# Cross-attention with masked image tokens: the setup of the first two query blocks in another order

## The reference

```python
text, ip_h = encoder_hidden_states[:, :end_pos], encoder_hidden_states[:, end_pos:]
q = _split_heads(hidden_states @ w_q, HEADS)
k, v = _split_heads(text @ w_k, HEADS), _split_heads(text @ w_v, HEADS)
out_text = _merge_heads(_sdpa(q, k, v))
mask_ip = _ip_mask(bbox, B, S, hidden_states.dtype)   # 0 or -10000 for each query and image token
k_ip, v_ip = _split_heads(ip_h @ w_k_ip, HEADS), _split_heads(ip_h @ w_v_ip, HEADS)
out_ip = _merge_heads(_sdpa(q, k_ip, v_ip, mask=mask_ip))
out = (out_text + out_ip) @ w_out + b_out + hidden_states
```

## Time and profile before

| | us |
|---|---|
| median of 3 runs (750.12 to 752.63) | 751.3 |
| the profiled execution | 747.52 |
| its span | 745.7 |
| PE busy | 690.5 (93%) |
| DVE busy | 537.3 (72%) |
| ACT busy | 288.2 (39%) |
| POOL busy | 213.6 (29%) |

### The profile page before, as it was taken

One profiled execution on the slowest core, in us unless ns is written; L12 is line 12 of the kernel. 1 busy time (PEld: TensorE's weight loads), 2 busy tenths in 40 slices (PEclk: granted clock), 3 DMA queues, 4 the chain that ended last, 5 costly groups with the idle time before them and its releaser, 6 DMA issues.

```text
span 745.7 us, 18922 instructions
## 1 busy us (share of the span) xinstructions
PE 690.5 (93%) x6410; PEld 630.2 (85%) x6410; DVE 537.3 (72%) x1686; ACT 288.2 (39%) x626; POOL 213.6 (29%) x359
## 2 busy tenths in 40 slices
PE   4977783899999999999999999999999999999987
PEld 3665363798999999999999999989898999999876
DVE  4342151978787888878787879797979787878764
ACT  1031112616262625353534444352626171616151
POOL 8100000523233231415050505051424242323323
PEclk9989796999999999999999999999999999999979
DMA  9946823335252625343434444444444343535220
GB/s 267 318 114 181 174 94 101 80 89 149 83 156 64 164 73 152 85 138 96 130 94 129 107 129 106 127 102 136 93 130 100 101 127 94 143 86 119 85 50 36
DMA packets 79543, 89.52 MB, mean 120 GB/s; under 512 B 10680, under 2 KB 63416, under 8 KB 79492
## 3 DMA queue, kind: packets, MB, share of 16 engines
q1 hardware_dynamic: 79016, 88.45, 43.6%
q10 hardware_dynamic: 492, 0.61, 0.3%
HBM read 39.21 MB, written 10.62 MB: 67 GB/s over the span
## 4 chain that ended last, share of the span: by engine, by line
PE 76%; DMA 8%; DVE 6%; SPq 6%; issue 2%; ACT 1%; ACTq 0%; POOL 0%; DVEq 0%
PE psum L1011 32%; PE psum L1112 10%; PE psum L1064 7%; PE psum L1096 6%; PE psum L1091 5%; DMA q_stack<-aux_a 5%; PE psum L1120 3%; PE psum L893 3%; PE psum L1121 3%; SPq L419 2%; DMA x_in<-in_x 2%; PE psum L1135 1%; PE psum L972 1%; PE psum L1118 1%; PE psum L962 1%
## 5 line engine op out<-in xcount | busy, mean ns | idle before, releaser
L795 DVE TENSOR_REDUCE neg_max<-psum 128x2 f32<-128x292 f32 x320 | 145.4, 455 | 86.6 <-PE psum L1064 86.4
L510 POOL TENSOR_TENSOR attn<-o_parts 128x128 f32<-128x128 f32 x160 | 73.9, 462 | 440.1 <-DVE o_parts L836 440.1
L1011 PE MATMUL psum<-wo_both,at_hi 128*128 128x320 f32 x640 | 153.2, 313 | 0.0
L1011 PE MATMUL psum<-xt_hi,wq_hi 128*128 128x256 f32 x400 | 115.7, 289 | 3.8 <-DVE xt_lo L763 3.8
L1064 PE MATMUL psum<-k_stack,q_stack 104*128 104x154 f32 x640 | 112.6, 287 | 2.5 <-DVE neg_max L796 1.2
L1011 PE MATMUL psum<-xt_hi,wq_lo 128*128 128x256 f32 x400 | 112.9, 282 | 0.0
L1011 PE MATMUL psum<-xt_lo,wq_hi 128*128 128x256 f32 x400 | 112.7, 282 | 0.0
L823 DVE TENSOR_TENSOR p_lo<-psum,p_hi 128x512 f16<-128x512 f32 x160 | 108.0, 683 | 2.7 <-ACT psum L647 2.4
L1011 PEld LDWEIGHTS psum<-wo_both,at_hi 128*128 128x128 f32 x640 | 109.6, 188 | 0.0
L645 ACT ACTIVATE p_hi<-psum 128x512 f16<-128x512 f32 x160 | 95.2, 595 | 27.8 <-PE psum L1091 27.7
L1112 PE MATMUL psum<-v_tail,p_tail 128*128 128x264 f32 x320 | 102.2, 401 | 2.6 <-DVE p_lo L823 1.6
(11 more groups left out here) (93 smaller groups left out, 1278.8 us busy)
## 6 DMA issues: line engine op xcount, KB each, us to landing
q_stack<-q_hi SPq DMA_DIRECT2D x128, 96.0 KB
x_in<-in_x SPq DMA_DIRECT2D x16, 640.0 KB, 4.1
x_res<-in_x SPq DMA_DIRECT2D x16, 640.0 KB, 5.1
out<-out_sb SPq DMA_DIRECT2D x32, 320.0 KB
q_stack<-q_hi SPq DMA_DIRECT2D x128, 64.0 KB
q_stack<-q_lo SPq DMA_DIRECT2D x64, 96.0 KB
q_stack<-q_lo SPq DMA_DIRECT2D x64, 64.0 KB
q_stack<-aux_a SPq DMA_DIRECT2D x48, 64.0 KB, 2.4
```

The costliest lines, as they stand in the source:

```text
L510: nc.gpsimd.tensor_tensor(cols, o_parts[:, qt, 0:4, :], o_parts[:, qt, 4:8, :], ALU.add).then_inc(att_half, 1)
L795: nc.vector.tensor_reduce(dst[:, :, 0], src[:, :, 0:TEXT], AX_X, ALU.max, negate=True)
L1011: last = nc.tensor.matmul(ps, l(c), r(c), start=(i == 0), stop=(i == len(terms) - 1))
```

## The change

1. **Context ahead of the mask chain.** On DVE the copies to `ctx_t` and `rest_t` come first, the comparisons in `small` after them. Waits stay the same.
2. **wq among the keys.** `wq_raw` is split (ACT high, DVE low) in parts 0 and 1 behind key group 3 and parts 2, 3 and 4 behind key group 4 (on ACT behind the mask's DMA, on DVE behind the mask values). The x of block 0 is then split without wq in between.
3. **x ahead of the image tokens' wv.** In SP's first XIN step the load of x of block 1 is issued before the load of `w_v_ip`.
4. **Batch 1's values behind the first maxima.** "ip" becomes unit 3 and is made ahead of S 1 1 0 in iteration 0; batch 1's two units become 4 and 5 and are made in iteration 1, ahead of S 3 0 0, S 3 1 0 and S 4 0 0. ACT copies them ahead of Q 1 and ST 0 2, DVE splits them behind S 4 0 0 and S 4 0 1, and PE waits for these splits ahead of ST 0 2. PE no longer waits for the sixth copy at the end of iteration 0.
5. **SP's tail of the setup in two pieces.** Ahead of iteration 1: keys of batch 1, `wo` (after 4 products), batch 0's 8 tail DMAs (after 4 copies). Behind the DMAs of AUX 0 of iteration 1: batch 1's 8 tail DMAs, the wait for all six products and both tails, and the bias.
6. `small` and `v_rest_ip` change places in SBUF, because `small` now lives until after the copies.

```diff
+W_Q_PLACES = {3: (0, 1), 4: (2, 3, 4)}
...
-V_UNITS = [("batch 0", 0, 512), ("batch 0", 512, D), ("rest", 0, D), ("batch 1", 0, 512), ("batch 1", 512, D), ("ip", 0, D)]
+V_UNITS = [("batch 0", 0, 512), ("batch 0", 512, D), ("rest", 0, D), ("ip", 0, D), ("batch 1", 0, 512), ("batch 1", 512, D)]
...
-    ("S", 1, 0, 1): ((3, 0, 3),), ("S", 1, 1, 0): ((3, 3, 6),), ("S", 1, 1, 1): ((3, 6, 8),),
-    ("S", 2, 0, 0): ((4, 0, 8),), ("S", 2, 1, 0): ((5, 0, 8),),
...
+    (0, "S", 1, 1, 0): ((3, 0, 8),), (1, "S", 3, 0, 0): ((4, 0, 4),), (1, "S", 3, 1, 0): ((4, 4, 8),),
+    (1, "S", 4, 0, 0): ((5, 0, 8),),
 }
+V_COPY_PLACES = {(0, "S", 0, 0, 0): (0, 1), (0, "S", 1, 0, 0): (2,), (0, "S", 1, 1, 0): (3,), (1, "Q", 1): (4,), (1, "ST", 0, 2): (5,)}
+V_SPLIT_PLACES = {(0, "S", 0, 0, 0): (0, 1), (1, "S", 4, 0, 0): (4,), (1, "S", 4, 0, 1): (5,)}
...
-            def rest_of_setup():
+            def before_aux():
 
                 keys_to_stack(1)
 
-                sp.wait_ge(s_vp, len(V_UNITS))
+                sp.wait_ge(s_vp, 4)
                 sp.dma_start(wo_raw[:, KC:2 * KC, :], wo.rearrange("(c p) n -> p c n", p=P)).then_inc(s_wo, 16)
                 sp.wait_ge(s_ones_all, BATCHES)
-                sp.wait_ge(s_vc, len(V_UNITS))
...
+                sp.wait_ge(s_vc, 4)
+                fill_tails(0)
+
+            def after_aux():
+
+                fill_tails(1)
+
+                sp.wait_ge(s_vp, len(V_UNITS))
                 sp.wait_ge(s_vt[0], 16 * 8)
                 sp.wait_ge(s_vt[1], 16 * 8)
...
+                        if isinstance(t, int) and t == 1 and n == 0:
+                            after_aux()
                     if kind == "XIN":
-                        if not it.back:
-                            sp.dma_start(w_v_ip, wv_ip.rearrange("(c p) n -> p c n", p=P)).then_inc(s_wv_ip, 16)
 
                         sp.wait_ge(xt_ready, t * NX + NX)
                         sp.dma_start(x_in[:], x_rows[bass.ds(t * QB + QB, QB), :].rearrange("(a p) d -> p a d", p=P)
                                      ).then_inc(x_loaded, 16)
+                        if not it.back:
+                            sp.dma_start(w_v_ip, wv_ip.rearrange("(c p) n -> p c n", p=P)).then_inc(s_wv_ip, 16)
...
+                for n in W_Q_PLACES.get(g, ()):
+                    w_high(n)
...
                     if (n, first) == (3, 0):
 
+                        pe.wait_ge(s_wv_ip, 16)
                         pe.wait_ge(s_vsplit, 1)
...
+                    if isinstance(t, int):
+                        make_values(V_PLACES.get((t, kind, *args), ()))
+                        if t == 1 and (kind, *args) == ("ST", 0, 2):
+
+                            pe.wait_ge(s_vsplit, 4 * V_PARTS)
...
                     pe.wait_ge(s_ktail, 4)
-                    pe.wait_ge(s_vc, len(V_UNITS))
```

More of the change, by code:

```diff
@@ L271, in attention_kernel @@
             pick = sb("pick", [16, BATCHES * IP], BF16, setup)
-            with ExitStack() as first:
-                small = sb("small", [16, 256], where=first)
-            v_rest_ip = sb("v_rest_ip", [P, GROUPS, DH], where=setup)
+            small = sb("small", [16, 256], where=setup)
         aux_rows = [sb("aux_a", [16 * len(SET_A), QB], F32R), sb("aux_b", [16 * len(SET_B), QB], F32R)]
@@ L455, in body @@
                 if not it.back:
-                    rest_of_setup()
+                    before_aux()
             iterations(sp, body)
@@ L536, in _, with w_high @@
                                      bank[2 * b][:].rearrange("p (c k) -> p c k", c=4), ACT.Copy).then_inc(s_ctx_t_act, 1)
+            def w_high(n):
+                if n < GROUPS:
+                    cols = slice(P * n, P * (n + 1))
+                    act.wait_ge(s_wq, 16)
+                    nc.scalar.activation(wq_hi[:, :, cols], wq_raw[:, :, cols], ACT.Copy).then_inc(s_wsplit_hi, 1)
+                else:
+                    c = n - GROUPS
+                    act.wait_ge(s_wo, 16)
+                    nc.scalar.activation(wo_hi[:, c, :], wo_raw[:, KC + c, :], ACT.Copy).then_inc(s_wsplit_hi, 1)
             for g in range(GROUPS):
@@ L558, in _ @@
                                      ACT.Copy, scale=SCALE).then_inc(s_khi, 1)
[L560 to L571 removed]
             def copy_values(units):
[L575 to L577 removed]
+                for n in units:
                     keys, c0, c1 = V_UNITS[n]
@@ L605, in x_high @@
                                      ).then_inc(xh_done, 1)
-            for n in range(GROUPS):
-                w_high(n)
-                if n < NX:
-                    x_high(n, n + 1, general[n])
+            for u in range(NX):
+                x_high(u, u + 1, general[u])
             def body(it):
@@ L618, in body @@
                     bank_a = general[it.general_bank(gen)]
-                    if not it.back:
-                        copy_values(V_PLACES.get((kind, *args), ()))
+                    if isinstance(t, int):
+                        copy_values(V_COPY_PLACES.get((t, kind, *args), ()))
                     if isinstance(t, int) and t == 1 and (kind, *args) in W_O_PLACES:
@@ L682, in _ @@
             nc.vector.tensor_copy(rest_t[:], rest).then_inc(s_ctx_t, 1)
+            dve.wait_ge(s_grid, 48)
+            nc.vector.tensor_copy(pick[0:9, :], small[0:9, 128:128 + BATCHES * IP])
+            nc.vector.tensor_scalar(gx, xs, box[:, 0:1], None, ALU.is_ge)
+            nc.vector.tensor_scalar(gy, ys, box[:, 1:2], None, ALU.is_ge).then_inc(s_msk, 1)
+            dve.wait_ge(s_msk, 1)
+            nc.vector.scalar_tensor_tensor(out=gx, in0=xs, scalar=box[:, 2:3], in1=gx, op0=ALU.is_le, op1=ALU.mult)
+            nc.vector.scalar_tensor_tensor(out=gy, in0=ys, scalar=box[:, 3:4], in1=gy, op0=ALU.is_le, op1=ALU.mult
+                                           ).then_inc(s_msk, 1)
             dve.wait_ge(s_ones_row, 1)
@@ L734, in w_low @@
                                             ).then_inc(s_wsplit, 1)
+            for g in range(GROUPS):
+                dve.wait_ge(s_khi, g + 1)
+                for b in range(BATCHES):
+                    last = nc.vector.scalar_tensor_tensor(
+                        out=k_lo[:, g, b, 0:TEXT], in0=k_bank(g)[:, b * TEXT:(b + 1) * TEXT], scalar=SCALE,
+                        in1=k_hi[:, g, b, 0:TEXT].bitcast(F32), op0=ALU.mult, op1=ALU.subtract)
+                last.then_inc(s_klo, 1)
+                if g in COUNTS:
+                    mask_values(*COUNTS[g])
+                for n in W_Q_PLACES.get(g, ()):
+                    w_low(n)
+            dve.wait_ge(s_khi, GROUPS + BATCHES)
+            for b in range(BATCHES):
+                last = nc.vector.scalar_tensor_tensor(
+                    out=k_lo[:, :, b, TEXT:CTX],
+                    in0=k_bank(K_IP_T)[:, 0:GROUPS * BATCHES * IP].rearrange("p (g b k) -> p g b k", g=GROUPS, b=BATCHES)[:, :, b, :],
+                    scalar=SCALE, in1=k_hi[:, :, b, TEXT:CTX].bitcast(F32), op0=ALU.mult, op1=ALU.subtract)
+            last.then_inc(s_klo, 1)
             def split_values(units):
-                for n, _, end in units:
+                for n in units:
                     keys, c0, c1 = V_UNITS[n]
-                    if keys in ("ip", "rest") or end < CC:
-                        continue
                     dve.wait_ge(s_vc, n + 1)
@@ L765, in x_low @@
                                         ALU.subtract).then_inc(x_freed, 1)
-            for n in range(GROUPS):
-                w_low(n)
-                if n < NX:
-                    x_low(n, n + 1, general[n])
+            for u in range(NX):
+                x_low(u, u + 1, general[u])
             def body(it):
@@ L858, in body @@
                                                 ).then_inc(out_done, 1)
-                    if not it.back:
-                        split_values(V_PLACES.get((kind, *args), ()))
+                    if isinstance(t, int):
+                        split_values(V_SPLIT_PLACES.get((t, kind, *args), ()))
             iterations(dve, body)
```

58 lines of the change are left out of this document (11 added, 47 removed), and 2 rows, old and new, of the table V_PLACES.

## The result

| | before | after |
|---|---|---|
| median of 4 runs, us | 751.45 (750.12 to 752.63) | 732.82 (729.49 to 735.33) |
| profiled execution | 747.52 | 729.49 |
| its span | 745.7 | 727.7 |

The changed kernel takes 0.975 of the time (95% interval 0.9706 to 0.9793): 18.6 us less on the medians, 18.0 us on the two spans, where 20.3 had been forecast. On the page of the profile after, PE's busy time has hardly moved; it now fills 95% of a shorter span. What went is idle time at the start.

A forecast was written before the change was run, and what follows sets the result against it. It took PE to bound the steady iterations, so only the start, up to iteration 1's first ST, could give anything; 1.5 + 0.8 + 17.0 + 0.2 + 0.8 = 20.3 us off 751.3 gave 731.0 us, range 724 to 738.

The forecast's parts named there:

- S 0 0 0 to AUX 0, +17.0: Iteration 0 up to AUX 0 of iteration 1: earlier x and batch 1's values moved out save 17.0 us.
- Context ahead of the mask chain, +1.5: At the start: keys begin 4.6 us earlier, the mask chain is held again; gain 1.5 us.
- the bound of -0.5: Lower bound for the context's copies going first: all gain lost and PE falls to 1.2 GHz in the gap.
- wq among the keys, +0.8: Ahead of the first Q: DVE saves 2.0 us, ACT's high parts cost 1.2; gain 0.8 us.
- The bound of 0: Lower bound for splitting wq among the keys: no gain if wq lands late.
- the bound of 2.7: Upper bound for splitting wq among the keys: 2.7 us if the first Q products run at 2.4 GHz.
- AUX 0 to ST, +0.2: Iteration 1 up to ST: batch 1's products and a DVE wait replace the DMA wait; gain 0.2 us.
- After ST, +0.8: Behind the first ST of iteration 1: gain 0.8 us, bounds 0 and 2.8, depending on PE's clock.
- the maxima's DMAs stay the bound: Rival at iteration 1's ST: the maxima land near 108 us, sum some 4 us smaller, 735.0 us; 10%.
- w_v_ip lands with the keys of batch 1: Rival in iteration 0: w_v_ip lands at 89.6, PE waits 10.1 us more ahead of "ip", 741.1 us; 5%.
- PE stays at 1.2 GHz: Rival from x of block 1 to ST: low clock costs 21.7 us more, 752.7 us; 2%.
- nothing comes of it: Rival: what is saved ahead of ST comes back behind it through DVE's load, 751 us; 3%.

The follow-up runs named there:

- x_first_alone: The kernel before with only one edit, x of block 1 loaded ahead of w_v_ip; 741.13 us.
- x_last: The changed kernel with w_v_ip loaded ahead of x of block 1 again; 742.13 us.
- mask_first: The changed kernel with DVE's mask chain ahead of the context's copies again; 730.74 us.
- pool_wq_behind: The changed kernel with POOL's casts held until DVE's mask chain is done and wq split behind the image keys again; 723.17 us.
- parts_345: The changed kernel with both the context's copies ahead of the mask chain and wq among the keys undone; 730.61 us.
- pool_waits: The changed kernel with one wait added: POOL begins its casts only when DVE's mask chain is done; 726.86 us.
- split_early: The changed kernel with DVE's split of unit 4 moved from behind S 4 0 0 to behind S 3 1 1; 730.42 us.

## Why the prediction was right, and where it wasn't

The time forecast was 731.0 us, in a range of 724 to 738; measured were 732.8. The bottleneck was read rightly, and the largest term carries the result.

- **What bounds the kernel.** Right. Behind ST the iterations take 621.28 us instead of 622.28; 17.0 of the 18.0 us lie ahead of that moment.
- **S 0 0 0 to AUX 0, +17.0.** Right: +16.6. Wait for x 0.95 us (0.9 forecast), X 0 and the first half of "rest" 2.2 us faster (2.4), wait for w_v_ip 1.71 (1.3), AUX 0 4.5 us behind "ip" (4.9). AUX 0 came at 88.86 and not at 84 to 85, but only because S 0 0 0 came 1.8 us later instead of 2.3 earlier. x_first_alone and x_last confirm the part of x from both sides, 10.7 us and 9.3.
- **Context ahead of the mask chain, +1.5.** This step failed: -0.8. Its times were right: first key product at 10.52 (10.65), mask matmuls at 19.86 (20.2), released by DVE. What failed is the price of the gap that was foreseen: that PE falls to 1.2 GHz in it stood only in the bound of -0.5, and the sum left the second group at 4.20 us. The mask matmuls came 1.8 us earlier, but they and the second group took 2.6 us longer than before (1.44 against 0.81 and 6.19 against 4.20), and 2.4 to 3.2 us longer in each of the four traces with such a gap. The rows had the sign of it: behind PE's 9.3 us of idle time the first half of "rest" took 4.09 us, the second 2.28. The 20.2 us for the mask matmuls was near the best case: in the other three traces of this start they came at 21.1 to 21.4.
- **wq among the keys, +0.8.** The second step that failed: -0.8. Its terms were right where the clock held (mask_first, 9.13 us from the image keys' first matmul to the first Q, against 10.07 and 10.08 in pool_wq_behind and parts_345, which have part 2 undone: +0.9). But PE's longer wait for the rows, 2.64 us instead of 1.53, was in the changed kernel, in pool_waits and in split_early followed by 2.1 us of low clock (10.87 us in all three; x_last, where the clock fell a little later, 10.50). The bound of 0 left this out; the bound of 2.7 spoke of the clock, and only in the gain's favour.
- **AUX 0 to ST, +0.2.** Right in its mechanism: ST was released by DVE's last split, 3.76 us of wait (4.0 forecast), and SP came in time. Mis-sized in one term: the profiled execution measured +2.2, since unit 4's first half ran at full pace, where 1.7 us of low clock had been forecast. That one is a matter of the run. Where unit 4's split was left in place, the gap was 17.56 and 17.59 us with V at 3.60, 19.03 with V at 4.89, and 20.11 to 20.31 us with V at 5.97 to 6.17, against 19.5 forecast. In four of these seven traces nothing was gained here, and 2.4 to 2.6 us of low clock stood where 1.7 had been put. The profiled execution was also the shortest of its four; its median is 3.3 us above it.
- **After ST, +0.8.** The number came out, +1.0, but isn't shown to be the change's: from the first ST to the end of the span the other kernels with ST's wait for the maxima took 622.56 and 622.89 us, and those with batch 1's values moved 621.22 to 624.33. In the pair itself 0.6 us are seen at the first ST (1.49 us instead of 2.08), where the clock had not yet fallen.
- **Rivals.** That the maxima's DMAs stay the bound, that w_v_ip lands with the keys of batch 1, that PE stays at 1.2 GHz, and that nothing comes of it, are excluded by the waits above and by the clock of 1.00 between 80 and 106 us.

The sum missed by -4.1 at the start and -0.4 up to AUX 0, and by +2.0 and +0.2 behind it, so that the errors partly cancelled; the +2.0 comes from the level of the clock in one execution. That the total was close says something for the term of x and of batch 1's values, and little for the other four.

The Trainium skill, "SBUF — State Buffer", section "Who interferes with whom", was what spoke against part 1. The trace agrees with its mutual exclusion of GpSimd and VectorE, here with 2.73 us for 32 elements a partition beside a cast and 0.22 us without it. It also says that whoever comes first holds the other; x_first_alone shows this side too, with POOL's two casts in 7.51 us instead of 5.47: the second cast took 4.82 us and the first 2.75, since L686 ran first.

## What to carry to other kernels

Moving work ahead of a late chain only moves the idle time if the chain's end doesn't move: look for what holds the chain itself, here another engine's copies that could begin 4 us later at no cost, and count the low clock that may follow a gap at its new place. When a wait on one engine is taken away, follow the order of the loads in the queue first; one exchange of two lines was worth 9 us, as much as all the rest. Work that has to be done somewhere can be cut into single matmul chunks and laid into idle time that another engine causes: here 4.2 us of products cost 1.9 to 2.7 us there and took 6.2 off the way behind it. And look at more than one trace before pricing an edit of 1 or 2 us: with the same start order, the same landmark moved by up to 5.5 us between executions.
